# Linear attention and an FP4 feed-forward on one core: the attention chain dealt out over other steps, the last batch's matrices in tiles of their own, and another order of the last pairs

## Time and profile before

| what | value |
|---|---|
| median of three runs | 631.04 us (630.25 to 631.48) |
| the profiled execution's own time | 630.21 us |
| its span | 628.4 us |
| PE matmul busy | 556.2 us (89%) |
| DVE busy | 565.3 us (90%) |
| ACT busy | 411.0 us (65%) |
| POOL busy | 240.6 us (38%) |
| mean granted TensorE clock | 0.974 of full |

### The profile page before, as it was taken

The page is one execution under the profiler, slowest core; times in us unless marked ns, Lnnn a source line. Parts: engine busy times, 40 slices in busy tenths (PEclk is TensorE's granted clock), DMA queues, the critical chain, the costliest instruction groups (busy, mean ns, idle before and its releaser), DMA issues.

```text
span 628.4 us, 15141 instructions
## 1 busy us (share of the span) xinstructions
PE 556.2 (89%) x4957; PEld 427.8 (68%) x4957; DVE 565.3 (90%) x1201; ACT 411.0 (65%) x884; POOL 240.6 (38%) x208
## 2 busy tenths in 40 slices
PE   0276889999999999999999888999999999999667
PEld 0253667677787777678787665778888676788555
DVE  6979899999989999999899997999999999976824
ACT  3475788767678777667677775767777776555320
POOL 4443143443323344434443342443533344223316
PEclk9967899999999999999999999999999999999898
DMA  7010000000001001111101111111101111141213
GB/s 238 17 35 17 18 19 18 18 18 19 19 32 37 18 2 52 52 53 52 52 2 52 52 56 52 51 53 51 28 26 52 52 35 34 37 152 34 67 49 137
DMA packets 17473, 29.15 MB, mean 46 GB/s; under 512 B 2672, under 2 KB 4848, under 8 KB 17392
## 3 DMA queue, kind: packets, MB, share of 16 engines
q1 hardware_dynamic: 17392, 28.13, 13.7%
HBM read 19.73 MB, written 8.39 MB: 45 GB/s over the span
## 4 chain that ended last, share of the span: by engine, by line
PE 41%; DVE 34%; issue 15%; ACT 4%; POOL 2%; DVEq 2%; DMA 1%; POOLq 0%; SPq 0%; ACTq 0%
PE GU L1322 17%; PE DS L1332 5%; DVE hg L880 4%; DVE hq L888 4%; DVE h L840 4%; PE G L1389 4%; DVE ham L847 3%; PE DS L1334 3%; PE TR L1284 3%; DVE y L899 2%; DVE xq L829 2%; PE GU L1342 2%; DVE xt L820 2%; DVE st L794 1%; DVE xam L804 1%
## 5 line engine op out<-in xcount | busy, mean ns | idle before, releaser
L1322 PE MATMUL GU<-wgu,xqT 128*128 128x352 f16 x1536 | 255.8, 317 | 11.0 <-DVE h L840 4.3
L1322 PEld LDWEIGHTS GU<-wgu,xqT 128*128 128x128 f16 x1536 | 148.7, 100 | 88.4 <-issue 8.7
L592 ACT ACTIVATE sil<-GU,wkap 128x352 f32<-128x352 f32 x128 | 70.8, 553 | 71.6 <-PE GU L1322 70.5
L515 POOL TENSOR_TENSOR ht<-h,hrr 128x1408 f32<-128x1408 f32 x32 | 82.9, 2589 | 84.1 <-DVE hrr L854 82.5
L1332 PE MATMUL DS<-wdT,hqT 128*128 128x256 f16 x704 | 88.5, 275 | 2.6 <-ACT hqT L599 2.6
L840 DVE SCALAR_TENSOR_TENSOR h<-GU,wkap,sil 128x352 f32<-128x352 f32 x128 | 69.4, 542 | 18.8 <-ACT sil L592 15.6
L888 DVE TENSOR_TENSOR hq<-hg,hs 128x704 f16<-128x704 f16 x128 | 77.0, 642 | 1.0
L471 POOL TENSOR_TENSOR rs<-ve,half 128x2 f32<-128x2 f32 x32 | 25.2, 787 | 136.2 <-DVE ht L877 122.3
L481 POOL TENSOR_TENSOR xnat<-xs,xnat 128x510 f16<-128x510 f32 (+1 forms) x32 | 37.0, 1156 | 99.5 <-DVE hq L888 94.4
L1332 PEld LDWEIGHTS DS<-wdT,hqT 128*128 128x128 f16 x704 | 66.9, 99 | 11.7 <-ACT hqT L599 2.9
L1342 PE MATMUL GU<-Mx,xnT 128*128 128x128 f16 (+1 forms) x648 | 59.9, 233 | 5.2 <-DVE Mx L980 4.5
(11 more groups left out here) (152 smaller groups left out, 932.7 us busy)
## 6 DMA issues: line engine op xcount, KB each, us to landing
xin<-in_L_attn_x SPq DMA_DIRECT2D x34, 256.0 KB, 2.9
xe<-in_L_attn_x SPq DMA_DIRECT2D x25, 256.0 KB, 2.8
out<-o SPq DMA_DIRECT2D x25, 256.0 KB, 2.1
algebra<-in_L_ffn_w_down SPq DMA_DIRECT2D x1, 704.0 KB, 6.4
gring<-in_L_ffn_w_gate SPq DMA_DIRECT2D x1, 640.0 KB, 4.6
gring<-in_L_ffn_w_up SPq DMA_DIRECT2D x1, 640.0 KB, 5.2
xs<-in_L_attn_x SPq DMA_DIRECT2D x2, 256.0 KB, 4.5
xt<-in_L_attn_x SPq DMA_DIRECT2D x2, 256.0 KB, 5.1
```

The source lines that it names most:

```text
L515: g.tensor_tensor(paired(ht[:, 0:2 * I]), paired(h[:, q]), spread(hrr[:, q], 4 * CB), ALU.mult).then_inc(S["ht_d"], 1)
L592: a.activation(sil[:, c], GU[:, c, 0, 0:CH], ACT.Silu, scale=wkap[:, 0:1]).then_inc(S["sil_d"], 1)
L1322: last = t.matmul(GU[:, c, m, 0:CH], xqT[:, k, j, 2 * a_ + kc], wgu[:, b_, kc, 2 * m + c], start=(z == 0 and kc == 0), stop=(z == 2 and kc ...
```

## The change

- The tables are rewritten. gram0 is cut into four parts and gram1 into two; the first part of gram0 stands in step 6 of the batch before. t1q, norms, raw, tailor, product and top move to later places; tailor's second half is a step "scale" of its own. Two more places exist, (0,3) and (0,4) on DVE, and 3 on PE beside 1.
- GpSimd's inv stands in step 3 between ht and o, in the last batch where it was.
- Wv is multiplied by gamma once, in own_basis; gt is gone. den is made from PSUM by two operations that add 256 in the same step. kap is the reciprocal of ktop, which carries the factor. As's part is read from PSUM and not from HLs.
- The last batch has its own Mx_end and its own column of unm, and its high_low waits for no y. Its top and high_low are asked at (3,0,1) and (3,0,3) and answered at (3,0,1) and (3,0,4), all in pair 32.
- The tail is written out: PE makes s of pairs 23 and 24, then the last hidden transposes of row 0, s of 25, transposes of row 1, down product of row 0, s of 26, down product of row 1, s of 27 to 31. DVE makes the y in order; ACT the last copies and silus.

```diff
-        ASKS = {(-3, 0, 2): "weights_q", (-3, 1, 2): "weights_k", (-2, 0, 2): "weights_v",
-                (-1, 1, 2): "gram0_first", (0, 0, 1): "gram0_last", (0, 1, 2): "gram1", (1, 0, 2): "turn", (1, 1, 2): "t1q",
-                (2, 0, 1): "t1k", (2, 1, 0): "norms", (2, 1, 2): "raw", (3, 0, 2): "tailor", (3, 1, 2): "product",
-                (4, 1, 0): "top", (5, 0, 0): "high_low"}
-        ANSWERS = {(-4, 1, 1): "own_basis", (0, 1, 0): "gram0", (1, 0, 1): "gram1", (1, 1, 0): "turn", (2, 0, 2): "squares",
-                   (2, 1, 1): "norms", (3, 1, 0): "tailor", (4, 0, 1): "product", (4, 1, 1): "top",
-                   (5, 0, 1): "high_low"}
-        COPIES = {(-3, 1, 0): "weights_q", (-2, 0, 0): "weights_k", (-2, 1, 0): "weights_v", (2, 0, 0): "t1q", (3, 0, 1): "raw"}
+                (-2, 1, 2): "gram0_0", (-1, 0, 1): "gram0_1", (-1, 1, 1): "gram0_2", (6, 1, 2): "gram0_0", (0, 0, 1): "gram0_3",
+                (0, 1, 2): "gram1_0", (1, 0, 0): "gram1_1", (1, 0, 2): "turn", (2, 0, 0): "t1q", (2, 0, 2): "t1k",
+                (2, 1, 2): "norms", (3, 0, 2): "raw", (3, 1, 2): "tailor", (4, 0, 2): "product", (4, 1, 2): "top",
+                (5, 0, 1): "high_low"}
+        ANSWERS = {(-4, 1, 1): "own_basis", (0, 1, 0): "gram0", (1, 0, 1): "gram1", (1, 1, 0): "turn", (2, 1, 0): "squares",
+                   (3, 0, 0): "norms", (4, 0, 0): "tailor", (4, 0, 3): "scale", (4, 1, 0): "product", (5, 0, 0): "top", (5, 0, 2): "high_low"}
+        COPIES = {(-3, 1, 0): "weights_q", (-2, 0, 0): "weights_k", (-2, 1, 0): "weights_v", (2, 0, 1): "t1q", (3, 1, 0): "raw"}
...
 ASKS_END
-                    (3, 0, 2): "top", (3, 1, 1): "high_low"}
+                    (3, 0, 1): "top", (3, 0, 3): "high_low"}
 ANSWERS_END
-                       (2, 0, 1): "norms", (2, 1, 2): "tailor", (3, 0, 1): "product", (3, 1, 0): "top", (4, 1, 2): "high_low"}
+                       (2, 0, 1): "norms", (2, 1, 2): "tailor", (2, 1, 3): "scale", (3, 0, 0): "product",
+                       (3, 0, 1): "top", (3, 0, 4): "high_low"}
...
 POOL iteration, after ht
+                last_batch = isinstance(b, int) and b == BATCHES - 1
+                if i == 3 and not last_batch:
+                    wait(pool, "nrm_d", b + 1)
+                    g.tensor_tensor(inv[:, :], nrm[:, :], half[:, :], ALU.pow).then_inc(S["inv_d"], 1)
...
 DVE answer
-                        v.tensor_copy(As[:, 1, 0:P], HLs[:, 1, 0:P])
+                        v.tensor_scalar(As[:, 1, 0:P], G[:, D:D + P], down, None, ALU.mult)
...
+                    for i in range(KD):
+                        last = v.scalar_tensor_tensor(den[:, i:i + 1], G[:, i:i + 1], inv[:, i:i + 1], width[:, :], ALU.mult, ALU.add)
+                    last.then_inc(S["cs_ev"], 1)
+                    wait(dve, "cs_ev", b + 1)
+                    v.reciprocal(den[:, :], den[:, :]).then_inc(S["den1"], 1)
+                if step == "scale":
...
-                    v.tensor_copy(ktop[:, :], G[:, 0:1]).then_inc(S["kap1"], 1)
-                    v.reciprocal(kap[:, :], G[:, 0:1]).then_inc(S["kap1"], 1)
-                    wait(dve, "kap1", 2 * b + 2)
-                    v.tensor_scalar(kap[:, :], kap[:, :], MTOP, None, ALU.mult).then_inc(S["kap_d"], 1)
+                    v.tensor_scalar(ktop[:, :], G[:, 0:1], 1.0 / MTOP, None, ALU.mult).then_inc(S["kap1"], 1)
+                    wait(dve, "kap1", b + 1)
+                    v.reciprocal(kap[:, :], ktop[:, :]).then_inc(S["kap_d"], 1)
...
+                    v.tensor_scalar(wqkv[:, 2], wqkv[:, 2], gam[:, 0:1], None, ALU.mult).then_inc(S["w_own"], 1)
+                    v.memset(width[:, :], float(D)).then_inc(S["eps_d"], 1)
...
-                    if step == "high_low":
+                    if step == "high_low" and not (isinstance(b, int) and b == BATCHES - 1):
...
 PE
+            def tail():
+                last = BATCHES - 1
+
+                def s_pair(e):
+                    p = e + LAGE
+                    for j in range(2):
+                        s_product(p, p % 2, j, last, e == PAIRS - PB and j == 0)
+
+                p, k, first = PAIRS + 1, (PAIRS + 1) % 2, PAIRS + 1 - LAGE
+                s_pair(first)
+                s_pair(first + 1)
+                for c in range(2):
+                    hidden_transposes(p, k, 0, c, False)
+                s_pair(first + 2)
+                for c in range(2):
+                    hidden_transposes(p, k, 1, c, False)
+                down_product(p, k, 0)
+                s_pair(first + 3)
+                down_product(p, k, 1)
+                for e in range(first + 4, PAIRS):
+                    s_pair(e)
```

More of the change, by code:

```diff
@@ L541, in iteration @@
                     x_divide(p, k)
-                if i == 2:
+                if i == 2 and last_batch:
                     wait(pool, "nrm_d", b + 1)
@@ L1155, in iteration @@
                     down_weights(0)
+                attention(0, 4)
                 if on["e"] and not on["m"]:
@@ L1169, in iteration @@
                     x_scales(p - 1, 1 - k, 3)
+                attention(0, 3)
                 if on["mb"]:
@@ L1200, in iteration @@
                 attention(1, 2)
+                attention(1, 3)
                 if on["m"]:
@@ L1203, in iteration, with tail @@
                     h_scales(p, k, 2)
-            drive(dve, iteration)
+            def tail():
+                for p in range(PAIRS + 1, PAIRS + LAGE):
+                    for j in range(2):
+                        e_mul(p, p % 2, j)
+            drive(dve, iteration, tail)
         @block.tensor
@@ L1338, in s_terms @@
                 slot = ring(xnT, e, TRING)
+                Mb = Mx_end if isinstance(e, int) and e >= PAIRS - PB else Mx
                 for i, (a_, b_) in enumerate(((1, 0), (0, 0), (0, 1))):
                     for kc in range(KD):
-                        last = t.matmul(bank, slot[:, j, 2 * a_ + kc], Mx[:, b_, kc, columns],
+                        last = t.matmul(bank, slot[:, j, 2 * a_ + kc], Mb[:, b_, kc, columns],
                                         start=(i == 0 and kc == 0), stop=(i == 2 and kc == KD - 1))
@@ L1376, in ask @@
                 tiles = TOKENS // P
-                if step in ("gram0_first", "gram0_last", "gram1"):
+                if step and step.startswith("gram"):
                     first = b * PB if isinstance(b, int) else own_value(pe, b * PB, PB, (BATCHES - 1) * PB)
-                    m = int(step == "gram1")
-                    n0, n1 = {"gram0_first": (0, PB), "gram0_last": (PB, tiles), "gram1": (0, tiles)}[step]
+                    m, part = int(step[4]), int(step[6])
+                    n0, n1 = part * tiles // (4 - 2 * m), (part + 1) * tiles // (4 - 2 * m)
                     wait(pe, "xlo", b * PB + n1 // 2)
                     wait(pe, "xhi", b * PB + n1 // 2)
-                    wait(pe, *(("gram_e2", 2 * b + 1) if m else ("mats", b)))
+                    if part == 0:
+                        wait(pe, *(("gram_e2", 2 * b + 1) if m else ("mats", b)))
                     if isinstance(b, int) and b == 0:
@@ L1474, in attention @@
                     if step:
-                        ask(b, step)
+                        ask(b + (i == PB - 2), step)
                 for j in range(2):
@@ L1494, in iteration @@
                     attention(j, 1)
+                    attention(j, 3)
                     if on["h"]:
-                        down_product(h_p, k, j)
+                        down_product(p, k, j)
                     if on["e"] and not on["m"]:
```

105 lines of the change are left out of this document (56 added, 49 removed).

## The result

The changed kernel takes 619.76 us (median of four, 619.48 to 620.78), the kernel before on the same chip 631.16 us (four, 630.25 to 631.48): ratio 0.9825 (0.9808 to 0.9842), 11.4 us faster. The forecast was 617.0 with a range of 610 to 625. The profiled execution took 619.48 us (span 617.7), 10.73 less than the profiled one of before (630.21).

What follows compares the result with a forecast made beforehand. PE and DVE were taken as within a few per cent of each other, the attention chain deciding which is late. Loop 6.1 - set-up 0.8 + end 8.7 = 14.0 us gained: 617.0 us median, range 610 to 625.

Steps and rivals of the forecast that it cites:

- The loop, PE: Batch loop on PE: with gram0 and gram1 split, PE begins the batch's fifth pair 2.1 us earlier, near 462.3.
- The sign that I had named: Loop: from first h of a batch's first pair to that of its fifth, some 68.5 us instead of 72.0.
- step 4: Fifth of a batch's eight pairs of row tiles: takes in tailor and scale, 18.6 us instead of 16.99, 1.6 lost.
- The loop, DVE: DVE's own work in a batch's first four pairs becomes 16.7, 16.9, 17.2, 15.7 us; As read from PSUM saves 0.3.
- The port: SBUF port shared by DVE and GpSimd, in the loop: moved inv costs 0.8 us, fifth pair of a batch 0.7.
- Set-up: own_basis before the loop: one added multiply of 512 fp32 elements on DVE, 0.8 us lost.
- The end: Kernel's tail: earlier last matrices start the last add at 614.3 instead of 624.66; 10.4 us less 1.7 for clock, 8.7.
- The sign "614 less the loop's 5.3": Kernel's tail: start of the last GpSimd add, expected at 614 less the 5.3 us won in the loop.
- The loop gives nothing: Rival, loop: added port waits reach their bounds and eat the gain, 623.1 us; chance 0.15.
- The low clock at the end: Rival, kernel's tail: clock stays low, 22 us of PE work cost 6 more, 623 us; chance 0.12.
- the late matrices: Rival, kernel's tail: last matrices come no earlier, the end keeps its 12.31 us after 611, 625.7 us; chance 0.03.
- the add on xt and xg in every pair: Rival, loop: add of o hits xt and xg every pair, slower, 634 to 655 us at worst; chance 0.04.

Runs made afterwards that it cites:

- those at the port: Three kernels on the changed kernel with the early gram0 answer: GpSimd's xnat held for both hq pairs, 616.03 us; add of o moved, 618.63; ham halved, 605.18.
- the two kernels of the end: Changed kernel with PE's tail order as before, 621.91 us; changed kernel with the last batch's matrices made late, behind y of pair 23, 623.06 us.

## Why the prediction was right, and where it was wrong

The time was 2.8 us over the forecast and in its range; the sizes of the terms were less good than that. In the profiled executions (616.2 forecast, 619.48 found) the loop gave 4.2 less, the end 1.2 more, and the set-up cost 0.2 more. (This execution lies 0.28 under its median and not 0.83, which makes the 3.3 of the executions the 2.8 of the medians.) So it is in part luck that the time came out so near: too much for the loop and too little for the end partly cancelled.

**The loop, PE: wrong.** Two steps failed. "Step 1 begins on PE at 408.02 + 1.76 = 409.8 instead of 411.5": I moved PE's end of gram1 and kept its start. That start is DVE's answer, which the change leaves in place, so PE's earlier arrival became idle time, 2.10 us where 0.69 had been. "In step 1 a half gram1 replaces t1q, no difference": true for PE's load, but the slack that should take it had gone into the stop and the clock. I named PE's stops for the clock at the end of the kernel only, and never asked what the clock does behind a longer stop in the loop. The run with spare matmuls puts 1.5 us a looped batch on the clock, the run with the early answer 3.5 us in all (0.6 of it xt's). The sign that I had named came: steps 0 to 3 took 70.67 us (466.67 - 396.00) and not 68.5, only 1.4 less than before. In the first batch they shortened by 3.3 of the 4.2 us foreseen. Counted from the first h of step 0, PE began step 4 after 66.8 us (462.80 - 396.00), where it had been 67.9 and the forecast was 65.8: 1.1 of the 2.1 us came. DVE reached it after 70.7 and not 68.5. The 1.9 us that the loop did give are not the spreading's either: the kernel with the old places has them too.

**The loop, DVE: right.** Own work of steps 0 to 3 was forecast 16.7, 16.9, 17.2 and 15.7 + 0.8 of port; the stretches have 16.71, 16.91, 17.07 and 16.39. Step 4 was forecast 18.6 long and was 18.39. The read of As from PSUM, the rows that spoke against a rule of the Trainium skill ("VectorE: DVE Perf Modes", Why PSUM operands drop a tier), can be read directly now. DVE's groups of the kernel after:

```profile
L938 DVE TENSOR_SCALAR algebra<-G 128x128 f32<-128x128 f32 x4 | 1.2, 292 | 0.1
...
L1009 DVE TENSOR_SCALAR wqkv<-wqkv,gam 128x512 f32<-128x512 f32 x1 | 0.5, 486 | 0.0
```

292 ns for what took 570 in the mean: the forecast of -0.3 us is right, and the form that the rule calls slower was the faster one here, because the other had to wait. The four copies of before took 226, 581, 720 and 751 ns; the fastest had no GpSimd operation beside it, the two slowest lay under the add of o. The read from PSUM took 0.29 us under the same add (415.94 in the kernel after). So without GpSimd the copy is the faster one, as the rule has it.

**The port: right in size.** I priced inv in step 3 at 0.8. GpSimd's timeline there has inv behind ht, then the add, and DVE's, in the fence after it, has xg under the add:

```profile
452.85 1.01 POOL L526 TENSOR_TENSOR inv<-nrm,half 128x4 f32<-128x4 f32 x1
453.82 1.39 POOL L537 TENSOR_TENSOR o<-y,xe 128x512 f32<-128x512 f32 x1
```

```profile
454.13 1.64 DVE L838 SCALAR_TENSOR_TENSOR xg<-xT,xt 128x512 f16<-128x512 f32 x1
...
481.03 1.60 DVE L903 TENSOR_TENSOR hq<-hg,hs 128x704 f16<-128x704 f16 x2
```

xg took 0.95 us more than in the kernel before. In step 4 the hq pair without top in front came to 1.60, forecast 1.54 (1.25 before), and xt to 0.83 (0.68 before): 0.5 us of port, of 0.7 forecast.

**Set-up: right.** 0.8 forecast, 1.0 found; the multiply took 486 ns and the block that holds it 0.54 more. The other half lies upstream, and I did not settle it. Nor is 1.0 a firm number: in the other kernels with this own_basis, those at the port left out, the first batch's step 0 came from 0.25 to 1.56 us later than before in the profiled executions.

**The end: mechanism right, size low.** kap came at 587.47 (588.5 forecast), and the last add started at 613.88 (before 624.66). Pair 31 began 0.83 us earlier than before, so on the held times of the forecast this is 588.3 and 614.7, and 614.3 was forecast for the add. The sign "614 less the loop's 5.3" missed with the loop. The kernel after, PE, DVE and POOL at the end:

```profile
587.47 0.16 DVE L987 RECIPROCAL kap<-ktop 128x1 f32<-128x1 f32 x1
587.69 0.66 PE L1484 MATMUL G<-id,mt 128*128 128x128 f32 x4 [0.45 <-DVE kap L987]
...
596.60 1.53 PE L1371 MATMUL GU<-Mx_end,xnT 128*128 128x256 f16 x12
...
606.51 6.71 PE L1371 MATMUL GU<-Mx_end,xnT 128*128 128x256 f16 x60
...
613.88 1.26 POOL L532 TENSOR_TENSOR xT<-y,xT 128x512 f32<-128x512 f32 x1
```

The stop of 4.96 us before the transposes is 0.45, and 60 matmuls remain of the block of 96. I took 10.4 us at full clock less 1.7 for a low stretch; the clock stayed at 1.00 and 9.94 was gained. The term of this sum that was mis-sized is the allowance of 1.7 us for the clock, which measured nothing (10.4 forecast without it, 9.94 found): I put it where the stops had been taken away, and a clock step fell due in step 0 of the looped batches, where a stop was made longer.

**Rivals.** "The loop gives nothing" comes nearest: 1.9 of 6.1 was left, and that without the new places; but it was PE's stop that ate the rest and not the port, the cause I had given it. The low clock at the end, the late matrices and the add on xt and xg in every pair did not come.

## What to carry to other kernels

When work is taken out in front of a wait, look up what ends the wait: if that stays where it was, move it too, or the work saved turns into idle time, and on TensorE the clock can fall behind it. Try an edit with and without its partner, since two edits that are worth 0 and 2 to 3 us alone were worth about 7 together. And where a DVE operation waits for GpSimd, try another kind of DVE operation beside it first: moving GpSimd's only picked another victim, both times here.

## What the runs showed of the hardware

- TensorE's clock fell from 2.4 to 1.2 GHz behind a stop of 2.10 us with nearly full work on both sides, and not behind the stop of 0.69 us in the same place. In the second batch the stops were 2.56 and 1.18 us, with the same outcome, and the two kernels of the end that keep the new places have the same stops (2.5 and 2.1 us) and drops. With twelve spare matmuls in the stop it stayed up. The drop cost 1.3 us in the first group alone (3.27 against 1.95). The length of the stop does not decide by itself: where the loop jumps back, PE stood 3.07 and 2.86 us in the kernel before and the clock stayed at 1.00 (368 to 388 us), while in the kernel after it stood 2.33 us there and the clock fell (0.91 over the same stretch).
- The Trainium skill ("TensorE: Matmul & The Clock Gate", Why this matters for your kernels) expects drops from idle gaps longer than 2.10 us; here gaps of 2.10 and 2.33 us were followed by one.
- A fp32 TENSOR_SCALAR of 88 elements from SBUF to SBUF waits for a two-operand operation of GpSimd: 0.21 us alone, 0.98 beside xt. A TENSOR_REDUCE of 704 elements beside xnat took 0.87 us, its time elsewhere. The Trainium skill ("SBUF — State Buffer", Who interferes with whom) puts the first into the class of operations that can take the lock and counts TENSOR_REDUCE among those that never contend, so rule and rows agree for both.
